# The V projection taken out of the attention groups: a first stage of its own, seven block products per pair of batches

## The chip, the cores and the metric

One core of one Trainium2 chip runs the whole program. TensorE (PE) does the matrix products into PSUM, ScalarE (ACT), VectorE (DVE) and GpSimd (POOL) copy, split and normalise, and SyncE (SP) issues every transfer between the chip's memory (HBM) and SBUF on one queue. The metric is the device time of one execution in microseconds: 1646.34 us is the median of three runs of the kernel before (1646.15 to 1647.33).

## The reference

Two residual layers over 32 batches of 128 x 1024 values in 32-bit floats. The first multiplies each batch by a 128 x 128 matrix picked by an index; the second is causal attention with 16 heads of 64 between four 1024 x 1024 projections.

```python
# x: (32, 128, 1024)
x1 = x + einsum('bct,bcd->bdt', x, L0_weights[conditions])      # layer 1
q, k, v = (einsum('bsd,ed->bse', x1, W) for W in (Wq, Wk, Wv))   # 16 heads of 64
q = q * min(cond_1, 4)                                          # one factor per batch
attn = softmax(where(causal, q @ k.T / sqrt(64), lowest))       # 128 x 128 per head
out = x1 + einsum('bsd,ed->bse', attn @ v, Wo)
```

## The kernel before

**Numbers.** Every product of 32-bit operands is made of three products of split operands: each operand is written as a high part (`XH`, `WH`, ...) and the rest (`XL`, `WL`, ...), and `three()` (L495 to L498) issues high x high, high x low and low x high into one PSUM bank. ACT writes the high part, DVE or POOL subtracts it from the source and so writes the low part.

**Time in steps.** All five engines walk the same list of ticks (`T_START` to `T_OUT`); every operation has a due step in a table (`step_at`, `l0_a`, `kh_ev`, ...), and an engine's program is what falls due on it, in order. A step of the projections is one `three()` with 512 columns: three matmuls of 128 x 512 that contract 128 of the 1024 input columns, so a block (128 output columns, or one batch of V) has 8 steps. The tables set only the order on each engine; what really holds an instruction is its semaphores. A late instruction holds all that stands behind it on its engine.

**Groups.** 8 groups of 4 batches. There are 16 attention stages of 96 steps: stages 0 to 7 do heads 0 to 7 of all groups, stages 8 to 15 heads 8 to 15. A stage has 4 V blocks (one per batch, 512 columns) and 4 pairs of a Q block and a K block (128 columns, two heads, of all four batches at once). The order is Q0 K0 V0 V1 V2 V3 Q1 K1 Q2 K2 Q3 K3; in stages 0 and 8 V comes first. Behind each K block, 5 steps later, stand the scores of its two heads for 4 batches (`p_SC`, 12 matmuls of 128 x 256), and 18 and 20 steps behind that the products with V (`p_PV`, again 12). Between them the softmax runs: DVE adds the mask and takes the maximum, ACT takes the exponential, DVE the reciprocal, POOL normalises, DVE turns P in 10 transposes of 32 x 32 blocks, ACT and POOL split it (`PTH`, `PTL`). I call the 16 steps of a Q and a K block with these 24 small matmuls a cell. Three cells of a stage stand right behind one another; the fourth has the V blocks behind it.

**Layer 1** of group j+1 is spread through stage j: for each half batch three matmuls with the picked matrix (`l0_a`, PE), a copy back (`x_tile`), four transposes (`l0_b`), and the split into `XH`, `XL`. The split x1 of a group is stored once (`X_store`) and read again for stages 8 to 15 (`X_load`). The opening does batch 0 before step 0 and batches 1 to 3 in steps 0 to 24.

**End.** The output projection of group 0 is done plainly (64 steps), that of the other 28 batches in pairs by seven block products instead of eight (28 steps per pair, `pe_product`, `sums`, `w_sum`), with weight sums that are prepared in attention stages (`O_split`, `O_add`).

Of the kernel before, what the change touches and what calls it, by code (L numbers as in the profile page):

```python
# [40 lines left out]
def cond_attention(nc, x, idx, cond, w0, wq, wk, wv, wo, mask_d, ident_d, out):  # L41
# [11 lines left out]
    with ExitStack() as ctx:  # L53
        def sb(name, shape, dt=f32):
            return ctx.enter_context(nc.sbuf_tensor("t_" + name, shape, dt))
# [32 lines left out]
        xr = [sb(f"xr{n}", [128, D]) for n in range(2)]  # L88

        with nc.sbuf_tensor("t_WR", [128, 2, 512], f32) as tile:  # L90
            WR = tile
        xh = sb("xh", [128, 512], f32r)
        xl = sb("xl", [128, 512], f32r)
        with nc.sbuf_tensor("t_WO", [128, 512], f32r) as tile:
            WO = tile
        wr = [sb(f"wr{n}", [128, 128]) for n in range(4)]
        wh = sb("wh", [128, 128], f32r)
        wl = sb("wl", [128, 128], f32r)
        PT = sb("PT", [128, GB, 256])
        PP = sb("PP", [128, GB, 2, 128])  # L100
# [1078 lines left out]
```

## Time and profile before

| | |
|---|---|
| median of 3 runs | 1646.34 us |
| the profiled execution | 1645.11 us |
| its span, first to last instruction | 1643.8 us |
| PE busy | 1630.0 us of the span (99%) |
| DVE / ACT / POOL busy | 912.1 / 746.8 / 588.1 us (55 / 45 / 36%) |
| granted TensorE clock, mean | 0.999 |
| moved by DMA | 221.81 MB, 135 GB/s in the mean |

The span is the time between the first and the last recorded instruction; the device time is 1.3 us more. Matmuls are pipelined: one is shown as 0.39 us long though the next starts 0.23 us later, so the distance from start to start is what a matmul costs. An engine's idle time is listed with what ended it; only PE's can matter much here, since PE carries nearly the whole chain.

### The profile page before, as it was taken

The numbers are of one execution on the slowest core, as the hardware profiler recorded it, in microseconds if no ns is written. First come the engines' busy times: TensorE is split into PE (matmuls) and PEld (weight loads), VectorE is DVE, ScalarE is ACT, GpSimd is POOL, SyncE is SP. The second block draws the span as 40 slices with busy tenths as digits, with TensorE's granted clock in tenths as the row PEclk, the third lists the DMA queues.
The fourth block names the chain that finished last, engine by engine and source line by source line (L and its number), as shares of the span: only waits on it lengthen the run. The fifth ranks groups of instructions, "written<-read, shape, count | busy, mean of one in ns | idle before, by whom it ended". The sixth has DMA issues, their size and how long they took to land.

```text
span 1643.8 us, 22438 instructions
## 1 busy us (share of the span) xinstructions
PE 1630.0 (99%) x7978; PEld 1370.2 (83%) x7978; DVE 912.1 (55%) x1870; ACT 746.8 (45%) x2085; POOL 588.1 (36%) x513
## 2 busy tenths in 40 slices
PE   9999999999999999999999999999999999999999
PEld 7788888888888888878888888888888888888887
DVE  6464646455464637466655556464747455555553
ACT  7464555555454645455444444343545332222221
POOL 2443333434342423342323232222333124555552
PEclk9999999999999999999999999999999999999999
DMA  8442323223141415244424233223221477545442
GB/s 273 179 161 83 149 81 131 97 96 141 60 162 71 167 47 237 65 124 152 150 68 163 90 133 133 92 116 96 116 77 39 167 280 278 178 155 173 171 160 84
DMA packets 91489, 221.81 MB, mean 135 GB/s; under 512 B 8690, under 2 KB 47858, under 8 KB 85234
## 3 DMA queue, kind: packets, MB, share of 16 engines
q1 hardware_dynamic: 91378, 220.38, 37.4%
q8 instruction: 63, 1.03, 0.3%
q14 instruction: 48, 0.39, 0.1%
HBM read 119.69 MB, written 100.66 MB: 134 GB/s over the span
## 4 chain that ended last, share of the span: by engine, by line
PE 93%; DVE 2%; POOL 1%; DMA 1%; ACT 1%; issue 1%; SPq 0%; ACTq 0%; DVEq 0%
PE p_PJ L496 23%; PE p_PJ L497 23%; PE p_PJ L498 23%; PE p_SC L497 4%; PE p_SC L498 4%; PE p_SC L496 4%; PE p_PV L496 2%; PE p_PV L498 2%; PE p_PV L497 2%; PE p_LP L496 2%; PE p_LP L498 2%; PE p_LP L497 2%; PE p_LP L570 1%; DVE t_PT L767 1%; DMA t_wr<-w 1%; POOL t_PTL L909 1%
## 5 line engine op out<-in xcount | busy, mean ns | idle before, releaser
L496 PE MATMUL p_PJ<-t_XH,t_WH 128*128 128x512 f32 x1024 | 404.3, 395 | 0.0
L497 PE MATMUL p_PJ<-t_XL,t_WH 128*128 128x512 f32 x1024 | 400.8, 391 | 0.0
L498 PE MATMUL p_PJ<-t_XH,t_WL 128*128 128x512 f32 x1024 | 399.6, 390 | 0.0
L767 DVE STREAM_TRANSPOSE t_PT<-t_PP 32x256 f32<-32x256 f32 x640 | 278.3, 435 | 16.3 <-POOL t_PP L905 8.2
L909 POOL TENSOR_TENSOR t_PTL<-t_PT,t_PTH 128x512 fp32r<-128x512 f32 x128 | 165.7, 1315 | 339.4 <-ACT t_PTH L710 339.1
L496 PE MATMUL p_PJ<-t_WH,t_XH 128*128 128x512 f32 x708 | 278.0, 393 | 1.3 <-DVE t_XL L792 1.3
L497 PE MATMUL p_PJ<-t_WL,t_XH 128*128 128x512 f32 x708 | 276.3, 390 | 0.0
L498 PE MATMUL p_PJ<-t_WH,t_XL 128*128 128x512 f32 x708 | 275.8, 390 | 0.0
L705 ACT ACTIVATE t_PP<-t_PP,t_st 128x128 f32<-128x128 f32 x512 | 198.7, 390 | 93.3 <-DVE t_st L829 93.3
L905 POOL TENSOR_TENSOR t_PP<-t_PP,t_st 128x512 f32<-128x512 f32 x128 | 133.4, 1044 | 270.7 <-DVE t_st L833 270.5
L498 PEld LDWEIGHTS p_PJ<-t_XH,t_WL 128*128 128x128 f32 x1024 | 192.5, 188 | 41.5
L496 PEld LDWEIGHTS p_PJ<-t_XH,t_WH 128*128 128x128 f32 x1024 | 193.1, 189 | 33.1
L497 PEld LDWEIGHTS p_PJ<-t_XL,t_WH 128*128 128x128 f32 x1024 | 193.5, 189 | 32.6
L498 PEld LDWEIGHTS p_PJ<-t_WH,t_XL 128*128 128x128 f32 x708 | 132.9, 188 | 28.4
L496 PEld LDWEIGHTS p_PJ<-t_WH,t_XH 128*128 128x128 f32 x708 | 133.1, 188 | 25.8 <-issue 1.5
L710 ACT ACTIVATE t_PTH<-t_PT 128x512 fp32r<-128x512 f32 x128 | 74.5, 625 | 176.2 <-DVE t_PT L767 176.2
L497 PEld LDWEIGHTS p_PJ<-t_WL,t_XH 128*128 128x128 f32 x708 | 133.3, 188 | 24.1
L823 DVE SCALAR_TENSOR_TENSOR t_PP<-p_SC,t_beta,t_mask 128x256 f32<-128x256 f32 x256 | 111.6, 477 | 74.5 <-PE p_SC L498 74.5
L803 DVE TENSOR_TENSOR t_KL<-p_PJ,t_KH 64x512 fp32r<-64x512 f32 x128 | 88.2, 689 | 92.9 <-ACT t_KH L689 90.1
L689 ACT ACTIVATE t_KH<-p_PJ 64x512 fp32r<-64x512 f32 x128 | 75.6, 591 | 110.7 <-PE p_PJ L498 108.8
L899 POOL TENSOR_TENSOR t_xl<-t_xr,t_xh 128x512 fp32r<-128x512 f32 x56 | 72.8, 1300 | 121.9 <-ACT t_xh L664 120.8
L792 DVE TENSOR_TENSOR t_XL<-p_LP,t_XH 128x512 fp32r<-128x512 f32 x58 | 40.1, 692 | 103.7 <-ACT t_XH L677 103.4
(210 smaller groups left out, 2528.4 us busy)
## 6 DMA issues: line engine op xcount, KB each, us to landing
xth_scratch<-t_XH SPq DMA_DIRECT2D x8, 2048.0 KB, 6.5
xtl_scratch<-t_XL SPq DMA_DIRECT2D x8, 2048.0 KB, 11.5
at_scratch<-t_AT SPq DMA_DIRECT2D x128, 128.0 KB, 1.8
t_XH<-xth_scratch SPq DMA_DIRECT2D x8, 2048.0 KB, 7.9
t_XL<-xtl_scratch SPq DMA_DIRECT2D x8, 2048.0 KB, 12.5
t_xr<-x SPq DMA_DIRECT2D x30, 512.0 KB, 3.7
...
```

The lines of the kernel that those rows point to most:

```text
L496: pe.matmul(bank, lh, rh, start=first, stop=False, skip_group_check=goes_on)
L497: pe.matmul(bank, lh, rl, start=False, stop=False, skip_group_check=goes_on)
L498: return pe.matmul(bank, ll, rh, start=False, stop=last, skip_group_check=goes_on)
L689: act.activation(KH[r, :, 128 * h:128 * h + 128], pj[r], ACT.Copy).then_inc(act_k, 1)
L705: act.activation(PP[:, u, h, :], PP[:, u, h, :], ACT.Exp, bias=st[:, 0, u, h:h + 1], scale=1.0, accum_out=st[:, 1, u, h:h + 1]).then_inc(a ...
L710: act.activation(PTH[:, u:u + 2], PT[:, u:u + 2], ACT.Copy).then_inc(act_pt, 1)
L767: m = dve.transpose(pt[32 * j:32 * j + 32, :, 32 * i:32 * i + 32], pp[32 * i:32 * i + 32, :, 32 * j:32 * j + 32])
L803: dve.tensor_tensor(KL[r, :, k], pj[r], KH[r, :, k].bitcast(f32), ALU.subtract).then_inc(dve_k, 1)
L823: dve.scalar_tensor_tensor(out=PP[:, u], in0=SC[u // 2][:, 256 * (u % 2):256 * (u % 2) + 256].rearrange("p (h k) -> p h k", h=2), scalar=b ...
L899: pool.tensor_tensor(xl[:], x_tile(bb)[:, h * 512:(h + 1) * 512], xh[:].bitcast(f32), ALU.subtract).then_inc(pool_xl, 1)
L905: pool.tensor_tensor(pp, pp, r, ALU.mult).then_inc(pool_n, 1)
L909: pool.tensor_tensor(PTL[:, u:u + 2], PT[:, u:u + 2], PTH[:, u:u + 2].bitcast(f32), ALU.subtract).then_inc(pool_pt, 1)
```

## The change

V of all heads and batches is now computed in a stage of its own, together with layer 1, before any attention. Its results are split and stored to HBM (`vh_d`, `vl_d`), and so is the split x1. Batches 0 to 3 are done plainly (64 steps, 8 blocks, `pe_plain_v`). The other 28 batches go in 14 pairs: two batches by the two halves of the input columns are a 2 x 2 block matrix, Wv another, and seven block products of 4 steps give what took eight (`pe_v_step`). Four sums of x blocks per pair are made on POOL (`pool_x_sum`) and split by ACT and DVE; four sums of Wv blocks are made once on DVE (`T_add`, from a second load of Wv) and split in steps 24 to 64. Results are gathered from PSUM by ACT and DVE into `GA` and `VR`, split into `VOH`, `VOL` and stored.

After 456 steps come 16 attention stages of 64 steps, four cells each and no V blocks. They load the V of their half of the heads (`V_load`, 2 MB a stage) and x1 (`X_load`, now 14 loads of 4 MB). Stage 0 takes the group that the V stage left in SBUF, stage 8 the one of stage 7. The Q and K weights are split in the V stage (first halves, `p_split`, two pieces in each of pairs 4 to 11) and in cells of the attention (second halves), stored, and loaded when needed (`W_load`). The splits of the output weights are spread over cells 19 to 57; their sums stand 6 steps ahead of their splits instead of 3. The end is the same.

```diff
-STEPS = 96
-T_END = NGRP * STEPS
+STEPS = 64
+PAIR = 28
+NP = B // 2
+T_SEV = 64
+T_ATT = T_SEV + PAIR * (NP - 2)
+T_END = T_ATT + NGRP * STEPS
+GROUP = (7, 0, 1, 2, 3, 4, 5, 6, 6, 7, 0, 1, 2, 3, 4, 5)
...
+        for p in range(2, NP):
+            t = T_SEV + PAIR * (p - 2)
+            plan_l0_pair(2 * p, t - 30)
+            plan_l0_pair(2 * p + 1, t - 16)
...
+        for c in range(4):
+            T_load.put((10, 13, 31, 50)[c], c)
+            for i in range(4):
+                t = (24, 33, 43, 59)[c] + i
+                T_add.put(t, (c, i))
+                T_high.put(t + 1, (c, i))
+                T_low.put(t + 2, (c, i))
+        for p in range(2, NP):
+            t = T_SEV + PAIR * (p - 2)
+            X_store.put(t - 4, p)
+            for i in range(4):
+                Z_add.put(t + (-4.5, -3, -1.25, 0.25)[i], (p, i))
+                S_high.put(t + (-1.25, 2.5, 9.5, 13.5)[i], (p, i))
+                S_low.put(t + (-0.25, 3.5, 10.5, 14.5)[i], (p, i))
+            for i in range(7):
+                for d in range(4):
+                    P_at.put(t + 4 * i + d, (p, i, d))
+            r_at.put(t + 4.25, p)
+            for i, d in enumerate((8, 16, 20, 24, 28)):
+                g_at.put(t + d + 0.25, (p, i))
+            for i, d in enumerate((12, 21, 25, 29)):
+                n = 2 * GB + 4 * (p - 2) + i
+                vh_ev.put(t + d + 0.25, n)
+                vl_ev.put(t + d + 1, n)
+                v_store.put(t + d + 2, n)
...
+        W_load.put(T_ATT - 23.5, (0, 0))
+        W_load.put(T_ATT - 15.5, (1, 0))
+        W_load.put(T_ATT + 5, (1, 1))
...
+        def pe_v_wait(p, i):
+            k = p - 2
+            if i in (0, 2, 5):
+                pe.wait_ge(dve_X, 4 * p + {0: 1, 2: 2, 5: 4}[i])
+            else:
+                pe.wait_ge(dve_S, 4 * k + {1: 1, 3: 2, 4: 3, 6: 4}[i])
...
+            elif i == 2:
+                pe.wait_ge(act_r, k + 1)
+            elif i in (3, 5, 6):
+                pe.wait_ge(dve_g, 5 * k + {3: 1, 5: 2, 6: 3}[i])
+            if k == 0 and i in (1, 3, 4, 5):
+                pe.wait_ge(dve_TL, 16)
+
+        def pe_v_step(p, i, d):
+            if d == 0:
+                pe_v_wait(p, i)
+            lh, ll = v_operand(p, i)
+            mm = three(v_bank(p, i)[:], lh[:, d], ll[:, d], WSH[i][:, d, :], WSL[i][:, d, :], i in (0, 1, 4) and d == 0, d == 3, i in (2, 3, 5, 6))
+            if d == 3:
+                mm.then_inc(pe_P, 1)
...
+        def sp_load_sums(c):
+            if c >= 2:
+                sp.wait_ge(dve_TL, (4, 12)[c - 2])
+            for place in range(4):
+                r0, c0 = 512 * (place // 2) + 128 * c, 512 * (place % 2)
+                sp.dma_start(raw_wv(c)[place], wv[r0:r0 + 128, c0:c0 + 512]).then_inc(l_T[c == 1], 16)
```

How the order moves on three engines. PE, a V block with half a batch of layer 1 among it, in attention stage 1 before (a V step names `t_WH,t_XH`, layer 1 names `p_LP`):

```order
L496 MATMUL p_PJ<-t_WH,t_XH 128x512
L497 MATMUL p_PJ<-t_WL,t_XH 128x512
L498 MATMUL p_PJ<-t_WH,t_XL 128x512
L496 MATMUL p_LP<-t_xh,t_wh 128x512
L497 MATMUL p_LP<-t_xl,t_wh 128x512
L498 MATMUL p_LP<-t_xh,t_wl 128x512
L496 MATMUL p_PJ<-t_WH,t_XH 128x512
L497 MATMUL p_PJ<-t_WL,t_XH 128x512
L498 MATMUL p_PJ<-t_WH,t_XL 128x512
```

and the end of block product 2 and the start of product 3 (counted from 0) of a pair of the V stage now (`t_SH`, `t_SL` are the split sums of x blocks, `t_WSH`, `t_WSL` the split Wv blocks and sums):

```order
L636 MATMUL p_SC<-t_WSH,t_XH 128x512
L637 MATMUL p_SC<-t_WSL,t_XH 128x512
L638 MATMUL p_SC<-t_WSH,t_XL 128x512
L636 MATMUL p_SC<-t_WSH,t_SH 128x512
L637 MATMUL p_SC<-t_WSL,t_SH 128x512
L638 MATMUL p_SC<-t_WSH,t_SL 128x512
L636 MATMUL p_LP<-t_xh,t_wh 128x512
L637 MATMUL p_LP<-t_xl,t_wh 128x512
L638 MATMUL p_LP<-t_xh,t_wl 128x512
```

The forms are the same; the whole list of PE has 7769 rows before and 7601 now (four transposes in a row are one row of it in both).

DVE, before, from the last V block of stage 0 on:

```order
L810 TENSOR_TENSOR t_VL<-p_PJ,t_VH 128x512
L797 TENSOR_TENSOR t_WL<-t_W,t_WH 128x512
L792 TENSOR_TENSOR t_XL<-p_LP,t_XH 128x4x128
L806 TENSOR_TENSOR t_QL<-p_PJ,t_QH 128x512
L792 TENSOR_TENSOR t_XL<-p_LP,t_XH 128x4x128
L803 TENSOR_TENSOR t_KL<-p_PJ,t_KH 64x4x128 x2
```

and now, from step 55 to the first pair (step 64), with the last sums of Wv blocks (`t_TS`) and their splits:

```order
L1025 TENSOR_TENSOR t_XL<-p_PV,t_XH 128x4x128
L1033 COPY t_XR<-p_PV 128x4x128
L1098 TENSOR_TENSOR t_TS<-t_TS 128x512 x3
L1102 TENSOR_TENSOR t_WSL<-t_TS,t_WSH 128x512
L1098 TENSOR_TENSOR t_TS<-t_TS 128x512
L1102 TENSOR_TENSOR t_WSL<-t_TS,t_WSH 128x512 x2
L1083 TENSOR_TENSOR t_SL<-t_SUM,t_SH 128x512
L1102 TENSOR_TENSOR t_WSL<-t_TS,t_WSH 128x512
L1086 TENSOR_TENSOR t_VOL<-p_PJ,t_VOH 128x512
```

Where a few splits stood between PE's blocks, the last eight operations on Wv sums stand close together just ahead of the first pair.

SP, before, in stage 2, a group's store of x1 among stores of attention results:

```order
L1114 DMA at_scratch<-t_AT 128x256 x2
L1099 DMA xth_scratch<-t_XH 128x4096
L1100 DMA xtl_scratch<-t_XL 128x4096
L1114 DMA at_scratch<-t_AT 128x256
L956 DMA t_xr<-x 128x1024
```

and now in the V stage, around the store of a pair's x1 (1 KB pieces in HBM rows of 16 KB):

```order
L1308 DMA xth_scratch<-t_XH 1024x1x256
L1308 DMA xtl_scratch<-t_XL 1024x1x256
L1315 DMA vh_scratch<-t_VOH 128x512
L1316 DMA vl_scratch<-t_VOL 128x512
L1331 DMA t_PR<-wq 128x512
L1502 DMA x_scratch<-t_XT 128x1024
L1281 DMA t_XT<-x 128x1024
L1315 DMA vh_scratch<-t_VOH 128x512
L1316 DMA vl_scratch<-t_VOL 128x512
```

The loads of the next batches and of the weights to split now stand behind stores of 2 MB of x1 and 0.5 MB of V.

## Rows read from the trace of the kernel before

**Rows 1.** The page: busy time of PE and the chain that ended last.

```profile
PE 1630.0 (99%) x7978; PEld 1370.2 (83%) x7978; DVE 912.1 (55%) x1870; ACT 746.8 (45%) x2085; POOL 588.1 (36%) x513
PE 93%; DVE 2%; POOL 1%; DMA 1%; ACT 1%; issue 1%; SPq 0%; ACTq 0%; DVEq 0%
```

**Rows 2.** Waits of PE, whole span: waiting line, releaser, us total, times, longest.

```profile
PE p_PV L496 <- POOL t_PTL L909: 4.4, 10, 1.4
PE p_LP L496 <- POOL t_xl L899: 2.0, 1, 2.0
PE p_PJ L496 <- DVE t_XL L792: 1.3, 1, 1.3
PE p_LP L496 <- DVE t_XL L792: 1.2, 2, 0.8
```

**Rows 3.** Timeline of PE in Q and K blocks: start, duration, instruction; 38 matmuls left out.

```profile
1306.85 0.40 PE L496 MATMUL p_PJ<-t_XH,t_WH 128*128 128x512 f32 x1
...
1315.70 0.39 PE L496 MATMUL p_PJ<-t_XH,t_WH 128*128 128x512 f32 x1
```

**Rows 4.** Timeline of PE in the opening: step 0 and step 32.

```profile
12.92 0.47 PE L496 MATMUL p_PJ<-t_WH,t_XH 128*128 128x512 f32 x1 [1.34 <-DVE t_XL L792]
...
41.88 0.39 PE L496 MATMUL p_PJ<-t_XH,t_WH 128*128 128x512 f32 x1
```

**Rows 5.** Windows: length, busy PE, PEld, DVE, ACT, POOL, clock, DMA share, GB/s.

```profile
10.00:15.00 5.00, 3.48 (x19) 2.62 (x18) 3.52 (x6) 4.62 (x10) 0.91 (x3) 1.00 1.05 393
25.00:30.00 5.00, 5.00 (x27) 4.15 (x27) 3.51 (x6) 3.67 (x8) 0.46 (x1) 1.00 0.69 215
35.00:40.00 5.00, 5.00 (x24) 4.16 (x23) 4.29 (x6) 3.51 (x7) 2.17 (x3) 1.00 0.93 247
55.00:60.00 5.00, 3.00 (x11) 2.10 (x10) 1.98 (x3) 3.19 (x7) 2.18 (x3) 0.84 0.36 126
1365.00:1385.00 20.00, 20.00 (x90) 16.56 (x89) 8.43 (x13) 4.47 (x8) 5.78 (x6) 1.00 0.84 322
943.38:957.20 13.82, 13.82 (x74) 11.88 (x73) 9.62 (x24) 7.53 (x26) 4.63 (x5) 1.00 0.53 223
```

**Rows 6.** The chain in order of time: the load of one picked matrix.

```profile
42.38 12.76 DMA t_wr<-w
```

**Rows 7.** Timeline of SP's queue, the stores issued ahead of it.

```profile
38.06 0.43 SPq L1099 DMA_DIRECT2D xth_scratch<-t_XH  x1
38.53 0.43 SPq L1100 DMA_DIRECT2D xtl_scratch<-t_XL  x1
```

**Rows 8.** Instructions by line and form: busy us, mean ns, idle before.

```profile
L792 DVE TENSOR_TENSOR t_XL<-p_LP,t_XH 128x512 fp32r<-128x512 f32 x58 | 40.1, 692 | 103.7 <-ACT t_XH L677 103.4
L853 DVE TENSOR_TENSOR t_XL<-t_Y,t_XH 128x512 fp32r<-128x512 f32 x28 | 18.0, 685 | 0.2
L853 DVE TENSOR_TENSOR t_XL<-t_WR,t_XH 128x512 fp32r<-128x512 f32 x14 | 19.7, 1444 | 8.7 <-ACT t_XH L744 8.7
L677 ACT ACTIVATE t_XH<-p_LP 128x512 fp32r<-128x512 f32 x58 | 34.7, 598 | 59.0 <-PE p_LP L570 58.1 <-POOL t_WL L948 1.0
L899 POOL TENSOR_TENSOR t_xl<-t_xr,t_xh 128x512 fp32r<-128x512 f32 x56 | 72.8, 1300 | 121.9 <-ACT t_xh L664 120.8
L933 POOL TENSOR_TENSOR t_PP<-t_PP 128x512 f32<-128x512 f32 x7 | 12.1, 1721 | 0.1
L915 POOL TENSOR_TENSOR t_xr<-t_xr 128x512 f32<-128x512 f32 x16 | 21.1, 1321 | 9.3 <-DVE t_xh L849 6.8 <-DVE t_xl L849 1.3
```

**Rows 9.** Timeline of POOL in a cell between two cells.

```profile
957.20 2.54 POOL L909 TENSOR_TENSOR t_PTL<-t_PT,t_PTH 128x512 fp32r<-128x512 f32 x2 [8.12 <-ACT t_PTH L710]
960.31 1.04 POOL L905 TENSOR_TENSOR t_PP<-t_PP,t_st 128x512 f32<-128x512 f32 x1 [0.57 <-DVE t_st L833]
```

**Rows 10.** Timeline of PE: the product with V that takes this `PTL`.

```profile
958.96 0.28 PE L496 MATMUL p_PV<-t_PTH,t_VH 128*128 128x256 f32 x1
```

More of the change, by code:

```diff
@@ new lines, in cond_attention, with slot @@
+        WSH, WSL = [None] * 7, [None] * 7
+        def slot(n, where):
+            WSH[n] = sb(f"WSH{n}", [128, 4, 512], f32r, where)
+            WSL[n] = sb(f"WSL{n}", [128, 4, 512], f32r, where)
+        with ExitStack() as early:
+            for n in range(3):
+                slot(n, early)
+            with nc.sbuf_tensor("t_W0a", [128, DC, 512], f32) as tile:
+                W0 = [tile]
+            slot(3, early)
+        WH, WL = [], []
+        for n in range(2):
+            WH.append(sb(f"WH{n}", [128, DC, 512], f32r))
+            WL.append(sb(f"WL{n}", [128, DC, 512], f32r))
@@ L84, in cond_attention @@
+        WEH = sb("WEH", [128, 4, 512], f32r)
+        WEL = sb("WEL", [128, 4, 512], f32r)
+        PT = sb("PT", [128, GB, 256])
+        xr = [sb(f"xr{n}", [128, D]) for n in range(2)]
+        PP = sb("PP", [128, GB, 2, 128])
         with nc.sbuf_tensor("t_LATE", [128, 4, 512], f32) as tile:
@@ L87, in cond_attention @@
         KL = sb("KL", [128, GB, 256], f32r)
[L88 to L100, printed above, removed]
+        QH = sb("QH", [128, T], f32r)
+        QL = sb("QL", [128, T], f32r)
         PTH = sb("PTH", [128, GB, 256], f32r)
@@ L222, in cond_attention @@
+        for n in range(2 * GB):
+            block("v", n)
+            for d in range(DC):
+                step_at.put(8 * n + d, ("v", n, d))
+            vh_ev.put(8 * n + 8, n)
+            vl_ev.put(8 * n + 8.75, n)
+            v_store.put(8 * n + 9.75, n)
         for d in range(DC):
@@ new lines, in cond_attention, with quiet @@
+        for p in range(2):
+            X_store.put((27, 48)[p], p)
+        def quiet(cell):
+            return T_ATT + 16 * cell + 21 + 9.5
+        p_load, p_split, W_load = At(), At(), At()
+        for m in range(16):
+            t = T_SEV + PAIR * (2 + m // 2) + (10.5, 23.25)[m % 2]
+            p_load.put(t - 9, m)
+            p_split.put(t, m)
+        for m in range(16, 32):
+            p_load.put(quiet(1) - 22 + 11 * (m - 16) if m < 18 else quiet(m - 16) + 2.5, m)
+            p_split.put(quiet(m - 14), m)
@@ L798, in dve_program @@
+                for m in p_split(tick - TICK):
+                    raw, high, low = qk_piece(m)
+                    dve.wait_ge(act_p, m + 1)
+                    dve.tensor_tensor(low, raw, high.bitcast(f32), ALU.subtract).then_inc(dve_p, 1)
                 for n in kl_ev(tick):
@@ new lines, in sp_load_W @@
+        def sp_load_W(n, part):
+            cols = slice(0, 512) if n % 2 == 0 else slice(256 * part, 256 * part + 256)
+            for low in range(2):
+                if n == 0 and low == 0:
+                    sp.wait_ge(s_p, 32 * 16)
+                if n < 2 and part == 0:
+                    sp.wait_ge(pe_P, 7 * (NP - 3) + 2 * n + low + 1)
+                elif n == 2 and low == 0:
+                    sp.wait_ge(pe_q, 4 * NG)
+                elif n == 3 and part == 0 and low == 0:
+                    sp.wait_ge(pe_k, 4 * NG)
+                to = (WH, WL)[low][n % 2][:, :, cols].bitcast(f32)
+                sp.dma_start(to, qk_half(n, low, cols)).then_inc(l_W_rest[n // 2] if part else l_W[n], 16)
@@ L1033, in sp_load_pair @@
         def sp_load_pair(q):
[L1034 to L1035 removed]
+            g, b = divmod(batches(q)[0], GB)
             if q == 0:
```

971 lines of the change are left out of this document (610 added, 361 removed).

## The prediction

> **What bounds the kernel now.** I read the page's busy times and its chain first: PE is busy 1630.0 us of 1643.8 and carries 93% of the chain, no other engine is over 55% [rows 1]. Then PE's waits: only some 9 us in the whole span [rows 2]. So the time is the number of matmuls times their distance. That is read from start to start, not from the 0.39 us shown: 39 matmuls in 1315.70 - 1306.85 = 8.85 us, 0.227 us for one of 128 x 512 [rows 3]; a step of three is 0.681 us. The opening gives the price of layer 1: 32 steps and batches 1 to 3 took 41.88 - 12.92 = 28.96 us [rows 4], less 32 x 0.681 = 21.79 leaves 2.39 us a batch. A cell of Q, K, scores and V products takes 13.82 us [rows 5], 10.9 of them in its 16 steps. The windows also show the clock: full, except 0.84 in the 5 us in which PE stood still for 2.0 us. Last come the queue (rows 6 and 7) and what the other engines have room for [rows 8 to 10].
>
> **What goes.** Steps: 1536 + 64 + 392 = 1992 before, 64 + 392 + 1024 + 64 + 392 = 1936 now. 56 x 3 = 168 matmuls of 0.227 us: **-38.1 us**. Each of 14 pairs has 84 in place of 96; nothing covers them, PE is the chain. Layer 1, scores, V products and the end keep their matmuls.
>
> Waits that go: the 4.4 us of V products for `PTL`, mostly where V or weight splits stood in DVE's and POOL's way; the 2.0 us of layer 1 for `xl` in the opening with about 0.8 us of clock behind it (0.16 of a 5 us window); the 1.2 us for `XL` banks, of which there are two now [rows 2, 5]. **-8 us** together; at the least 0, if others take their place. The 2.0 us came from the queue: the load of one picked matrix took 12.76 us to land [rows 6], since two stores of 2 MB were issued 4 us ahead of it [rows 7]. It is issued 21 steps ahead of its product now, not 12.
>
> **What comes, in the V stage.** A pair has 28 steps and two batches of layer 1: 84 x 0.227 + 2 x 2.39 = 23.8 us. The others must do in that time:
> - ACT: 4 `xh`, 4 copies back, 4 `XH`, 2 raw copies, 1 gather, 4 sums, 4 V, at most 2 weight pieces, 25 x 0.60, and two small ones: 15.6 us.
> - DVE: 4 `XL`, 2 raw, 5 gathers, 4 sums, 4 V, 2 pieces, 21 x 0.69 = 14.5 us; nine of these take both inputs from SBUF.
> - POOL: 4 `xl` of 1.30, 4 sums of 1.32 to 1.72 and small ones: 12.5 to 14 us [rows 8].
>
> All fit. The tightest links are those between products in one bank, 4 steps = 2.7 us for a gather of 0.69; ahead of it DVE has at most an `XL` and a raw copy, 1.4. And product 1 has 4 steps after the sums' chain of POOL, POOL, ACT, DVE. I count 1.5 us for odd delays in 14 pairs; none at best; if every pair lost 1 us, 14.
>
> DVE's two-input operations have two prices here, 685 ns and 1444 ns for the same form, the long one in the stretch where POOL computes sums beside it [rows 8]. If all nine pay the long price, DVE has 14.5 + 9 x 0.76 = 21.3 us in 23.8: it still fits, but every link gets thinner. I take 14.5 to 18, since POOL is busy about half the time; the long price is part of the first rival. The Trainium skill (SBUF — State Buffer, on the shared port pair) says that a VectorE instruction with two SBUF inputs contends with a GpSimd instruction that reads SBUF; by it the 21.3 us would be the rule wherever POOL has work, and the rows of 1444 ns agree.
>
> **The sums of Wv, once.** They come just ahead of the first pair, and product 1 of that pair waits for all 16 splits, at step 68. The last load (1 MB) is issued at step 50, behind a store of 2.1 MB of x1 and one of 0.5 MB of V. At 322 GB/s at 0.84 busy, so 383 at full [rows 5], the 3.6 MB take 9.5 us, at 0.83 us a step to step 61.5 or 62. Behind it DVE has eight operations on sums and one more, nine of 0.69 = 6.2 us = 9 steps: step 71. PE is then 3 to 4 steps late: **+2.6 us**, and a clock loss like the one above, +0.8. Bounds: nothing, if the load lands by 59; 6 us, if the queue is as slow as in the window of 247 GB/s at 0.93.
>
> **The queue.** Per pair: x 1.05 MB, picked matrices 0.13, x1 stores 1.05, split x1 2.10, V 2.10, and in 8 pairs the weight pieces 1.57: 8.0 MB there, 6.4 in the other six. The rate at full share is 374 to 383 GB/s in two windows (393 at 1.05, 322 at 0.84), 312 in one (215 at 0.69) and 266 in the worst (247 at 0.93) [rows 5]. The form new here, 1 KB pieces stored, isn't in the trace; those windows are my bounds. I take about 350, nearer to the mass of rows: 22.9 us for 8.0 MB, under 23.8. The backlog is then largest after the x1 store, some 3 MB or 9 us; an x load issued there lands 10 steps later and is due after 12. So it is hidden, narrowly. The Trainium skill (DMA: Bandwidth & Descriptors, Bandwidth) lists 341 GB/s for a transfer of 1 MB and asks for at least 1 MiB each; here V goes in pieces of 256 KB. With its 341 the pair's bytes would take 23.5 us, hidden as well.
>
> **The start of attention.** The first Q block needs 4.2 MB of weights, issued at steps 4.5 and 8 of the last pair behind some 2 MB: 6.3 MB at 383 are 16.5 us = 24 steps of 0.681, due at 28. The K weights are due 8 steps later and have 8.4 MB ahead and with them. Both nearly on time: **+1 us**; 0 to 6.
>
> **The cells.** All 64 are now back to back. The trace has that already: three in each stage follow one another, and there `PTL` is ready at 957.20 + 1.27 = 958.47 and taken at 958.96, 0.5 us to spare [rows 9, 10], with DVE busy 9.6 of 13.8 us [rows 5]. So the cadence holds without V. In 16 cells a sum of output weights (1.32 us on POOL, [rows 8]) now stands ahead of the normalising at 960.31, which has a gap of 0.57 before it [rows 9]: 0.75 us late there, 0.25 at the second one, within 0.5. Weight splits fall in gaps of DVE. **+1 us**; 0 to 16 x 0.75 = 12. X, 4.2 MB, and V, 2.1 MB, per stage of 55 us are 115 GB/s: no load there.
>
> **Sum**, from the profiled execution's own 1645.1 us: -38.1 - 8 + 1.5 + 3.4 + 1 + 1 = -39.2, so 1605.9. Its time is 1.2 us under the median of the runs, inside their spread; I say **1606 us**.
>
> **The rivals.**
> 1. *The V stage is paced by more than PE, mildly* (queue at 312 GB/s or DVE by the shared port). 8.0 MB at 312 are 25.6 us, 1.8 over PE's, in 8 pairs 15 us: about 1620. For it: a backlog of 9 us in every pair, in-order engines, loads due 2 steps after they land. Against: the faster windows, and six pairs that need only 270 GB/s.
> 2. *The cells lose their 0.5 us.* If each cell waits 0.5 us more for `PTL`, since nothing between stages lets DVE catch up: 64 x 0.5 = 32 us, 1638. For it: ten such waits before. Against: the third cell in a row before had the same spacing as the second, 13.8 us.
> 3. *Slower than before: the queue at its worst rate.* At 266 GB/s 8.0 MB take 30.1 us, 6.3 over, times 8 = 50, and 6.4 MB take 24.2, 2 more in six pairs: 1658. It decides from 277 GB/s downward, where 8 x 5.1 us eat the 40. For it: one 5 us window, with pieces of 2 KB and 512 B. Against: it is a stretch of loads waiting for one another as much as a rate.
> 4. *No change*: the seven products save nothing because PE waits in every pair for the gathers, 2.8 us of the 23.8. Every link has over 1 us to spare, so I see no place for it.
>
> **How the numbers follow.** Forecast 0.64 (its own range 1599 to 1613), rival 1 0.18, rival 2 0.09, rival 3 0.06, rival 4 0.03. The range from 1598 to 1634 leaves out rivals 3, 4 and most of 2, and a little below: 0.2. A measurement here tells 0.2% (3.3 us) from no change: faster 0.91, same 0.02, slower 0.07.
>
> **What would show it.** PE's list 168 matmuls shorter and PE still at 98% or more; pairs of 23.8 us; the attention at 64 x 13.82 = 884 us with waits for `PTL` of 0.3 us here and there; one wait of 2 to 4 us at product 1 of the first pair, at about 70 us, with a dip of the clock. In the V stage the DMA share should stand at 0.85 to 0.95 for 8 pairs. I am wrong if PE waits there once per pair, for `xl`, `xh` or a gather behind a late load (rivals 1 and 3), or if the distance of cells is over 14.1 us (rival 2).

## The result, and the profile after

| | before | after |
|---|---|---|
| median (4 runs each, same chip) | 1646.84 us (1646.15 to 1649.08) | 1631.25 us (1630.27 to 1631.86) |
| span of the profiled execution | 1643.8 us | 1629.4 us |
| granted TensorE clock, mean | 0.999 | 0.995 |
| moved by DMA | 221.81 MB | 353.99 MB |

The ratio is 0.9902, 95% interval 0.9885 to 0.992: 15.6 us faster, where 40 were forecast. The time lies in the range of 1598 to 1634, in its upper end; in size the forecast is 25 us off.

The page of after, busy times and chain:

```profile
PE 1595.2 (98%) x7810; PEld 1340.5 (82%) x7810; DVE 1068.2 (66%) x2072; ACT 808.7 (50%) x2199; POOL 662.3 (41%) x554
PE 79%; DMA 6%; SPq 6%; DVE 3%; issue 2%; POOL 2%; ACT 2%; ACTq 0%; DVEq 0%
```

Against [rows 1] the list is 168 matmuls shorter, as said, and 34.8 us less busy. But the chain has 79% PE where it had 93: DMA and SP's queue carry 12% of it. PE's waits, whole span (against [rows 2]):

```profile
PE p_PJ L636 <- DVE t_VOL L1086: 5.1, 1, 5.1
PE p_LP L770 <- ACT t_XT L897: 4.8, 4, 3.1
PE p_PJ L636 <- DMA t_WL<-wl_scratch: 4.8, 1, 4.8
PE p_PV L636 <- DVE t_VR L1051: 4.2, 3, 2.0
PE p_PV L636 <- POOL t_PTL L1240: 2.3, 3, 1.1
PE p_PJ L636 <- DVE t_VR L1051: 2.0, 2, 1.7
PE p_PJ L636 <- ACT t_GA L905: 1.9, 3, 0.6
...
PE p_SC L636 <- ACT t_GA L905: 1.5, 3, 0.6
```

The waits that were to go are gone but for 2.3 us of `PTL`. In their place stand others, nearly all before or at the start of the attention. Without a wait it would begin at 13.74 + 456 x 0.681 + 31 x 2.39 = 398.4 us; its first matmul starts at 426.85. **28.5 us are lost in three places**, read as the distance from start to start above its price; the places below were read one by one, so their sum is not exactly that.

*The opening, 11 us.* PE around the last steps before the first pair, and its product 1:

```profile
74.04 0.39 PE L638 MATMUL p_PJ<-t_WSH,t_XL 128*128 128x512 f32 x1
77.49 0.66 PE L770 MATMUL p_LP<-t_ident,t_XT 128*128 128x128 f32 x4 [3.06 <-ACT t_XT L897]
83.27 0.77 PE L636 MATMUL p_PJ<-t_WSH,t_SH 128*128 128x512 f32 x1 [5.12 <-DVE t_VOL L1086]
83.84 0.63 PE L637 MATMUL p_PJ<-t_WSL,t_SH 128*128 128x512 f32 x1
84.26 0.63 PE L638 MATMUL p_PJ<-t_WSH,t_SL 128*128 128x512 f32 x1
```

The waits give 0.9 + 3.2 + 5.4 us in distances, and the matmuls behind stand 0.43 us apart up to 86: 1.4 us more, at the lower of the two clock levels (1.2 GHz). The cause of both waits is seen in SP's queue and on DVE and ACT: the load of Wv's last quarter is issued at 64.79 and awaited until 74.14, and the copies of x stand behind the sums on ACT.

```profile
64.79 2.66 SPq L1302 DMA_DIRECT2D t_TS<-wv  x4
```

```profile
74.14 2.15 DVE L1098 TENSOR_TENSOR t_TS<-t_TS 128x512 f32<-128x512 f32 x3 [6.58 <-DMA t_TS<-wv]
...
77.41 2.63 DVE L1102 TENSOR_TENSOR t_WSL<-t_TS,t_WSH 128x512 fp32r<-128x512 f32 x2
79.96 1.75 DVE L1083 TENSOR_TENSOR t_SL<-t_SUM,t_SH 128x512 fp32r<-128x512 f32 x1
...
82.49 0.68 DVE L1086 TENSOR_TENSOR t_VOL<-p_PJ,t_VOH 128x512 fp32r<-128x512 f32 x1
```

```profile
74.87 2.08 ACT L918 ACTIVATE t_WSH<-t_TS 128x512 fp32r<-128x512 f32 x3 [8.65 <-DVE t_TS L1098]
```

From the landing to the end of `t_VOL` DVE takes 9.0 us for ten operations. Those that take both inputs from SBUF took up to 1.75 us each while POOL was at work beside them (77.8 to 81.2 us); all others took about 0.7. Product 1 also waits for this `t_VOL`, the last plain V block, whose bank it writes. It stands behind the sums on DVE, and product 1 starts 0.10 us after its end, at 83.17.

*The pairs, 13 us.* All from 182 to 327 us, in pairs that carry weight pieces: twelve waits, 9.8 us, eleven of them 11.4 in distances, and some 2 at the lower clock near 327. Pairs there take 25.5 us (five pairs in 310.19 - 182.48), not 23.8. *The start of the attention*: 4.84 us for the low first weights, 5.0 in distance, and another 1.9 behind it at the lower clock. Windows of after, columns as in [rows 5]:

```profile
40.00:60.00 20.00, 20.00 (x94) 16.56 (x93) 19.35 (x26) 11.32 (x21) 6.37 (x6) 1.00 1.04 333
60.00:80.00 20.00, 14.31 (x68) 11.15 (x66) 11.39 (x18) 10.50 (x22) 10.89 (x10) 0.99 1.07 363
80.00:100.00 20.00, 16.73 (x73) 13.80 (x74) 10.76 (x16) 9.11 (x19) 7.19 (x7) 0.84 0.63 200
182.48:327.11 144.63, 134.85 (x624) 107.92 (x623) 87.59 (x118) 77.44 (x151) 75.98 (x66) 1.00 0.98 310
420.00:440.00 20.00, 15.16 (x58) 12.06 (x58) 2.61 (x5) 1.77 (x4) 0.00 (x0) 0.83 0.88 306
```

Line four is the main reading: for 145 us the 16 DMA engines are 98% busy and move 310 GB/s. 8.0 MB a pair at 310 are 25.8 us, what a pair takes. No engine is near its limit there: DVE 88 us of 145. How a late transfer reaches PE is seen on ACT, which takes its work in order. Its longest waits from 182 to 327 us are for the weight pieces and for the picked matrices (`t_wr`, which POOL prepares):

```profile
ACT t_PRH L924 <- DMA t_PR<-wk: 17.1, 5, 6.1
ACT t_wh L892 <- POOL t_wr L1220: 11.4, 6, 2.8
ACT t_PRH L924 <- DMA t_PR<-wq: 9.2, 2, 4.6
```

What stands behind such a wait is late, and DVE behind it: ahead of PE's 2.0 us at 224 us ACT waited 4.6 us for a piece and 2.8 for a matrix, and DVE 5.1 us for ACT. The full queue is seen in SP too: with much outstanding an issue takes 1.2 us and not 0.4, and SP becomes late itself.

```profile
254.97 1.26 SPq L1339 DMA_DIRECT2D wl_scratch<-t_PRL  x1
256.28 1.23 SPq L1315 DMA_DIRECT2D vh_scratch<-t_VOH  x1
257.55 1.24 SPq L1316 DMA_DIRECT2D vl_scratch<-t_VOL  x1
258.83 1.18 SPq L1331 DMA_DIRECT2D t_PR<-wk  x1
```

*The attention* keeps its cadence; the answer to [rows 9], POOL of a cell and of the next one, 13.81 us later:

```profile
1012.29 2.54 POOL L1240 TENSOR_TENSOR t_PTL<-t_PT,t_PTH 128x512 fp32r<-128x512 f32 x2 [8.12 <-ACT t_PTH L952]
1015.40 1.04 POOL L1236 TENSOR_TENSOR t_PP<-t_PP,t_st 128x512 f32<-128x512 f32 x1 [0.57 <-DVE t_st L1136]
...
1026.10 2.54 POOL L1240 TENSOR_TENSOR t_PTL<-t_PT,t_PTH 128x512 fp32r<-128x512 f32 x2 [8.12 <-ACT t_PTH L952]
```

### The profile page after: what moved, and what is told of

Its sections match the earlier page's. It is cut to its first block, busy times and chain, and to the rows that moved or that the text cites. A ratio compares the mean times of both kernels' runs of the same rounds, so it can differ in the third digit from the quotient of the medians.

```text
span 1629.4 us, 22999 instructions
## 1 busy us (share of the span) xinstructions
PE 1595.2 (98%) x7810; PEld 1340.5 (82%) x7810; DVE 1068.2 (66%) x2072; ACT 808.7 (50%) x2199; POOL 662.3 (41%) x554
## 2 busy tenths in 40 slices
DMA packets 171815, 353.99 MB, mean 217 GB/s; under 512 B 13234, under 2 KB 97458, under 8 KB 161458
## 4 chain that ended last, share of the span: by engine, by line
PE 79%; DMA 6%; SPq 6%; DVE 3%; issue 2%; POOL 2%; ACT 2%; ACTq 0%; DVEq 0%
PE p_PJ L636 19%; PE p_PJ L637 19%; PE p_PJ L638 18%; PE p_SC L637 4%; PE p_SC L636 4%; PE p_SC L638 4%; PE p_PV L636 2%; PE p_PV L637 2%; PE p_PV L638 2%; DMA t_wr<-w 2%; DMA at_scratch<-t_AT 2%; DMA t_WL<-wl_scratch 1%; SPq L1316 1%; PE p_LP L637 1%; PE p_LP L636 1%
## 5 line engine op out<-in xcount | busy, mean ns | idle before, releaser
L636 PE MATMUL p_PJ<-t_XH,t_WH 128*128 128x512 f32 x1008 | 395.5, 392 | 4.8 <-DMA t_WL<-wl_scratch 4.8
L638 PE MATMUL p_PJ<-t_XH,t_WL 128*128 128x512 f32 x1008 | 392.9, 390 | 0.0
L947 ACT ACTIVATION_READ_ACCUMULATOR t_PP<-t_PP,t_st 128x1 f32 x512 | 95.9, 187 | 0.0
L1132 DVE TENSOR_REDUCE t_st<-t_PP 128x2 f32<-128x256 f32 x256 | 94.2, 409 | 0.0
L1228 POOL TENSOR_TENSOR t_xl<-t_XT,t_xh 128x512 fp32r<-128x512 f32 x56 | 79.8, 1425 | 5.4 <-ACT t_xh L840 5.2
L1220 POOL TENSOR_TENSOR t_wr<-t_wr,t_ident 128x128 f32<-128x128 f32 x32 | 21.6, 676 | 143.6 <-DMA t_wr<-w 143.6
L1136 DVE RECIPROCAL t_st<-t_st 128x4 f32<-128x4 f32 x128 | 22.8, 178 | 87.2 <-ACT t_PP L947 87.2
L636 PE MATMUL p_PV<-t_PTH,t_VH 128*128 128x256 f32 x256 | 72.1, 282 | 2.3 <-POOL t_PTL L1240 2.3
L638 PE MATMUL p_PV<-t_PTH,t_VL 128*128 128x256 f32 x256 | 72.3, 282 | 0.0
L638 PE MATMUL p_SC<-t_KH,t_QL 128*128 128x256 f32 x256 | 72.2, 282 | 0.0
```

What stands on the lines that cost most here:

```text
L636: pe.matmul(bank, lh, rh, start=first, stop=False, skip_group_check=goes_on)
L638: return pe.matmul(bank, ll, rh, start=False, stop=last, skip_group_check=goes_on)
L947: act.activation(PP[:, u, h, :], PP[:, u, h, :], ACT.Exp, bias=st[:, 0, u, h:h + 1], scale=1.0, accum_out=st[:, 1, u, h:h + 1]).then_inc(a ...
L1132: dve.tensor_reduce(st[:, 0, u, :], PP[:, u], AX, ALU.max, negate=True).then_inc(dve_m, 1)
L1228: pool.tensor_tensor(xl[h][:], x_tile(bb)[:, h * 512:(h + 1) * 512], xh[h][:].bitcast(f32), ALU.subtract).then_inc(pool_xl, 1)
```

## Experiments

Each run has four timed executions of the kernel (e10 has ten), and before beside it on the same chip (medians 1646.1 for e1 to e4, 1645.0 for e5 to e8, 1646.3 for e9 to e12, 1647.8 for e13 to e16). The number to beat is after's 1631.3. "Waits in the pairs" are PE's from 180 to 330 us, 9.8 us in after.

**e1: the first weights in halves.** As K's do, Q's first 2 x 2 MB come in two parts of 2 x 1 MB each.

```diff
+        W_load.put(T_ATT + 3, (0, 1))
         W_load.put(T_ATT + 5, (1, 1))
```

> The first Q weights (4.2 MB, 512 columns) are loaded as two halves of 256 columns, the second half 3 steps after the start of attention; all else as in the changed kernel, whose span is 1629.4 us with a wait of 4.84 us at that start and some 2 us of half clock behind it. Queue theory: what is due at that moment is halved, the wait and the clock loss go, about 1624 us (-7). Rival: the transfer in front of it (stores of V and x1) is what is late, and the wait only moves to the K weights or shrinks to 3 us: 1628 to 1630.

1634.5 us (1631.6 to 1638.1), ratio 0.9932 (0.991 to 0.9954). The wait for `t_WL` fell to 0.7 us, and one of 3.5 us for low V came 29 us later:

```profile
428.92 0.47 PE L638 MATMUL p_PJ<-t_XH,t_WH 128*128 128x512 f32 x1 [0.66 <-DMA t_WL<-wl_scratch]
...
457.37 0.36 PE L638 MATMUL p_PV<-t_PTH,t_VH 128*128 128x256 f32 x1 [3.49 <-DMA t_VL<-vl_scratch]
```

The time lies above both forecasts: no gain. What was let past PE's first need was paid at its next.

**e2: the low half of V is not stored.**

```diff
-            sp.dma_start(vl_d[half][g][:, cols], VOL[n % 2][:].bitcast(f32)).then_inc(s_V[n % 2], 16)
```

> The low part of V is computed but not stored, and the load of it takes the high part, so the result is off; every engine's arithmetic is as in the changed kernel and a pair has 1.05 MB less in the queue (7.0 and 5.4 MB for 8.0 and 6.4), the opening 2.1 MB less. Queue theory (bytes at some 320 GB/s): the waits of the first pair (9 us), of the 8 pairs with weight pieces (12 us) and half of that at the start of attention go, with their clock losses: 1605 to 1612 us. Engine theory (ACT, DVE and POOL have too much to do in order): the waits stay, 1627 to 1631.

1609.2 us (1608.6 to 1609.6), ratio 0.9772 (0.9755 to 0.9788). With 1.05 MB of 8.0 less in a pair, and all work of the engines kept, PE waits for nothing from 180 to 330 us:

```profile
180.00:330.00 150.00, 150.00 (x710) 123.92 (x709) 101.52 (x133) 88.85 (x170) 88.02 (x76) 1.00 0.86 290
```

6.95 MB in 23.8 us are 292 GB/s, which the queue gives at 0.86 busy. The engines' work is kept, so that work is not what holds the pairs. But SyncE also has 4 of a pair's 22 issues less, so e2 alone does not part bytes from issues. The 22 us are most of the miss of 25; what it still loses is the opening (4.9 us for `VOL` again).

**e3: the weight pieces are not split.** Loaded and stored twice as they are; no ACT, no DVE.

```diff
-            sp.wait_ge(act_p, m + 1)
-            sp.dma_start(wh_d[m // 8][:, cols], high.bitcast(f32)).then_inc(s_p, 16)
+                sp.wait_ge(l_p[m % 2], 16 * (m // 2 + 1))
+                sp.dma_start(wh_d[m // 8][:, cols], raw).then_inc(s_p, 16)
...
-                sp.wait_ge(dve_p, m)
+                sp.wait_ge(s_p, 32 * m)
```

> The first 16 Q and K weight pieces are loaded and stored twice as they are, without ACT's copy and DVE's subtraction (the result is off); bytes and transfers are the same. Engine theory: ACT and DVE are freed of the two operations per pair and of ACT's waits for the piece (30 us in all), the 12 us of waits in the 8 pairs go, 1617 to 1620 us. Queue theory: at most a little, 1627 to 1632, since the loads of x and of the picked matrices come as late as before.

1635.3 us (1634.5 to 1636.6), ratio 0.993. DVE does 79 us of work in the 150 instead of 92, and PE still waits 7.6 us there:

```profile
180.00:330.00 150.00, 142.31 (x647) 113.74 (x645) 78.98 (x107) 73.91 (x145) 77.20 (x69) 0.98 0.90 304
```

Less work on the engines brought no gain, as the queue theory has it. The test is not clean, though: since the raw tile is now stored itself, SyncE holds its queue before each load of a piece until the last stores have landed (the last two lines of the edit). After has no such wait, and with it the DMA share fell to 0.90:

```profile
SPq L1335 <- DMA wl_scratch<-t_PR: 33.4, 12, 3.5
```

So it is e2, not e3, that rules out DVE's load and its shared port as what holds the pairs.

**e4: the split x1 stored in pieces of 8 KB.** As many bytes, from another tile that lies contiguous. The load of the first weights waits for these stores.

```diff
-            for tile, to in ((XH[0], xth_d), (XL[0], xtl_d)):
+            for tile, to in ((WSH[0], xth_d), (WSL[0], xtl_d)):
```

> The store of a pair's split x1 (2 x 1 MB) takes its bytes from a tile that lies in one piece (8 KB per partition on both sides, in place of 8 pieces of 1 KB), so the values stored are others; bytes, order and waits are the same. Piece-size theory: the queue gains speed, DMA share in the 8 pairs falls from 1.0 to some 0.85 and most waits go, 1608 to 1615 us. Byte theory: rate and waits stay, 1627 to 1632.

1622.9 us (1621.8 to 1623.4), ratio 0.9853 (0.9837 to 0.9869). Between both: larger pieces for 2.1 of the 8.0 MB are worth 8 us; 324 GB/s, and 3.9 us of waits in the pairs.

```profile
180.00:330.00 150.00, 145.98 (x685) 118.53 (x683) 97.22 (x127) 85.42 (x165) 86.28 (x74) 1.00 0.96 324
```

**e5: the sixteen pieces spread over pairs 1 to 12.** `PLACE` is a table of pair and half for each piece.

```diff
-            t = T_SEV + PAIR * (2 + m // 2) + (10.5, 23.25)[m % 2]
+            t = T_SEV + PAIR * PLACE[m][0] + (10.5, 23.25)[PLACE[m][1]]
```

> The sixteen weight pieces (0.8 MB each: read, then stored as high and low) come one or two to a pair over pairs 1 to 12, instead of two in each of pairs 4 to 11; nothing else changes. Theory (the queue gives some 320 GB/s, and a pair with two pieces has 8.0 MB for it, 25.0 us of queue in 23.8 us): eight pairs had to pay some 13.5 us; with one piece a pair has 7.2 MB, 22.5 us, and pays nothing, and the four pairs that keep two (2, 6, 9 and 12) stand apart, so their backlog is worked off. 1620 to 1625 us, and PE's waits for t_GA and t_VR, 9.6 us in the changed kernel, fall to under 3. Rival (a piece's own conversions on ScalarE and VectorE hold the evictions; there are as many of them as before): 1629 to 1633.

1628.6 us (1626.2 to 1630.2), ratio 0.9888. The waits in 180 to 330 us fell to 3.7, but the wait for the first weights grew from 4.8 to 6.3 us, since the queue is now fuller up to the end of the stage (0.93 busy from 330 to 420 us, 0.86 in after). Part of the gain was given back there: a miss of 4 us.

**e6: sums of Wv's quarters 0 to 2 on GpSimd, X of pair 1 stored at step 56.**

```diff
+                for c, i in T_add(tick):
+                    if c < 3:
+                        T_sum(pool, pool_TA, 4 * c + i, c, i)
...
-            X_store.put((27, 48)[p], p)
+            X_store.put((27, 56)[p], p)
```

> The sums of Wv's quarters 0 to 2 go from VectorE to GpSimd, two steps apart and begun 3 steps earlier; those of quarter 3 stay; and the X of the second pair is stored at step 56, behind the load of quarter 3, not at step 48 ahead of it. Theory (VectorE, busy 19.35 of 20 us at 40 to 60, and the late quarter 3 set the end of the sums, and TensorE waits 5.1 us for them at product 1 of the first pair, 3.1 us for X's evictions ahead of it, and then runs at the lower clock for 3 us): 8 to 10 us of the 10.9 go, and 1622 to 1625 us. Rival 1 (only the load of quarter 3 counts, and comes late as before behind the rest of the queue): the wait stays at 3 to 5 us, 1629 to 1632. Rival 2 (GpSimd's sums of 128x512 take so long, or hold VectorE back so much, that they are late themselves): the wait grows, 1633 to 1640.

1632.9 us (1630.0 to 1634.6), ratio 0.9918: no gain, between rivals 1 and 2. POOL was 19.8 of 20 us busy at 40 to 60, the load of quarter 3 was issued at 67.0 (64.8 in after), and product 1 waited 5.3 us.

**e7: high V stored from ScalarE's queue.** Same bytes, same pieces, another issuer.

```diff
                 for n in vh_ev(tick):
                     act_v_high(n)
+                    act.wait_ge(act_v, n + 1)
+                    act.dma_start(vh_d[half][g][:, b * 512:(b + 1) * 512], VOH[n % 2][:].bitcast(f32)).then_inc(s_V[n % 2], 16)
```

> The stores of V's high half are issued by ScalarE, behind its own eviction, and no longer by SyncE; bytes and pieces are the same. Theory (bytes and pieces set the rate; that SyncE's issues grow from 0.35 to 1.2 us is only the sign of a full queue): 1629 to 1635 us, the waits stay within 2 us of the 9.6 us for t_GA and t_VR, and ScalarE's issues get long in their turn. Rival (the length of the issues on one sequencer sets what is stored late): with 128 of some 300 issues off SyncE the waits for t_GA and t_VR fall below 4 us, and the time to 1618 to 1625.

1622.9 us (1621.8 to 1623.7), ratio 0.9856 (0.9827 to 0.9884). The theory that bytes and pieces alone set the rate fell; the rival's number came. The rate rose to 331 GB/s at the same busy share (309 to 315 at 0.97 to 0.99 in after and in e1, e6, e9, e12 and e15, each once), the waits in the pairs fell to 2.2 us, and no issue of ScalarE's was over 0.35 us, while SyncE's stayed long:

```profile
180.00:330.00 150.00, 147.79 (x696) 120.33 (x695) 98.12 (x129) 89.77 (x171) 89.56 (x76) 1.00 0.98 331
```

```profile
253.02 0.33 ACTq L915 DMA_DIRECT2D vh_scratch<-t_VOH  x1
```

```profile
258.28 1.32 SPq L1319 DMA_DIRECT2D vl_scratch<-t_VOL  x1
```

The edit changes three things at once: the issuer, the hardware queue that carries these bytes (queue 10 with 11.6% of the DMA engines' time, where after has all on queue 1), and the moment, for a high half now goes without waiting for VectorE's low half. The runs do not tell them apart. If 4 issues fewer on SyncE are worth at most these 8 us in e2 as well, at least 14 of its 22 are its bytes (an estimate).

**e8: e5, e6 and e1 together.**

> Three edits together: the pieces spread over pairs 1 to 12, the Wv sums of quarters 0 to 2 on GpSimd with the second pair's X stored later, and the first attention weights loaded in halves. If the first two losses stand apart, as the theory has it, their gains add: 1631.3 less 8 for the spread, less 8 for the sums, nothing for the halves, is 1615, range 1611 to 1619. If one backlog of the queue runs through all of it (what is not lost in the opening is lost in the pairs, for the queue is what is full from 40 us on): 1622 to 1630.

1628.7 us (1625.1 to 1631.6), ratio 0.9893: no more than e5 alone, in the range of the one backlog. Two of the three gave nothing by themselves, so it says little on whether gains add.

**e9: the X of the last pair stored in the attention.** SyncE waits for it before the X load of stage 2.

```diff
-            X_store.put(t - 4, p)
+            X_store.put(T_ATT + 12 if p == NP - 1 else t - 4, p)
```

> The X of the last pair (2 MB) is stored 12 steps into the attention, behind the loads of the first attention weights, of V and of X of the next group, and no longer 4 steps ahead of its pair's products. Theory (at the start of the attention the queue is a line: what stands ahead of the first weights' low half delays it; 2.1 MB at 340 GB/s are 6.2 us, more than the 4.8 us that TensorE waits): the wait for t_WL goes, the 2 us at the lower clock behind it too, 6 to 7 us less than the changed kernel run beside it. Rival (the wait moves on to the load of low V, as it did when the weights were loaded in halves, 3.5 us there): 2 to 4 us less. Rival (nothing: the weights are late from their buffers, not from the queue): within 1.5 us.

1629.6 us (1625.4 to 1631.3), ratio 0.9895. The wait for the weights fell from 4.84 to 1.68 us, and no lower clock followed (1.00 from 420 to 440, 0.83 in after); `PTL` then cost 1.1 at 483 us and as much once more before 900, where e12 has none. The median gains 2.1 us over e12 beside it, less than the 6 to 7 of the theory; the intervals overlap.

```profile
423.35 0.47 PE L636 MATMUL p_PJ<-t_XH,t_WH 128*128 128x512 f32 x1 [1.68 <-DMA t_WL<-wl_scratch]
```

**e10: X of pairs 0 and 1 stored behind the loads of Wv.**

```diff
-            T_load.put((10, 13, 31, 50)[c], c)
+            T_load.put((10, 13, 30, 49.5)[c], c)
-                t = (24, 33, 43, 59)[c] + i
+                t = (24, 33, 42, 59)[c] + i
-            X_store.put((27, 48)[p], p)
+            X_store.put((34, 56)[p], p)
```

> In the opening the X of pairs 0 and 1 is stored at steps 34 and 56, behind the loads of Wv's quarters 2 and 3, not at 27 and 48 ahead of them (2 MB each), and quarter 2's sums one step earlier. Theory (the chain load 2, sums 2, load 3, sums 3 sets product 1 of the first pair; each load waits behind 2 MB of X in the queue, 9 to 10 us from issue to landing where 1 MB alone would take 3): load 2 lands some 3 us earlier, load 3 as much or more, and of the 8.6 us of waits at 74 to 83 us 4 to 7 go: 4 to 8 us less than the changed kernel beside it. Rival (VectorE's own line of sums, 19.4 of 20 us busy at 40 to 60, is the limit, and each load waits for it through its buffer): 0 to 2 us less.

1637.9 us (1632.7 to 1644.9), ratio 0.9951: slower than after by 6. Pair 2's x takes the tile that pair 0's store reads. With that store later its low part is late, and layer 1 stands still ahead of a wait of 5.0 us that stayed:

```profile
63.00 0.76 PE L636 MATMUL p_LP<-t_xh,t_wh 128*128 128x512 f32 x1 [5.99 <-DVE t_XL L1025]
```

**e11: e5, e7, e9 and e10 together.**

> Four edits together: the last X stored late, X stored behind Wv's loads in the opening, high V stored from ScalarE's queue, and the weight pieces spread over pairs 1 to 12. If the three places are losses of their own: 6 for the start of the attention, 5 for the opening, and 10 to 12 of the 13.5 in the pairs, so 21 to 23 us less than the changed kernel beside it, 1607 to 1611 us, which is what the kernel would take if the queue cost nothing but the opening's rest. If they share one backlog, and relief at one place is paid at the next: 1615 to 1621.

1623.8 us (1622.2 to 1625.3), ratio 0.986: with e10's loss in it.

**e12: the changed kernel again**, the measure for e9 to e11.

> The changed kernel itself, unedited, on the chip of the other three, so that edits worth 3 to 7 us are read against it and not over two chips: 1631 us, 1628 to 1634.

1631.7 us (1631.0 to 1634.4), ratio 0.9915 (0.9899 to 0.9932), with the three places as in after: 4.9 us at product 1, 5.0 for the weights.

**e13: e5, e7 and e9.**

> The four edits of the kernel with all cures, but for the one in the opening, which cost 6.2 us by itself against the changed kernel beside it: so the last X stored late, high V stored from ScalarE's queue, and the weight pieces spread. If the edits' gains add (2 us, 8 to 9 us and 3 us by themselves): 1617 to 1619 us. If the spread and ScalarE's queue cure the same thing: 1620 to 1623.

1620.2 us (1617.8 to 1621.1), ratio 0.9828 (0.9808 to 0.9848): the median fits the second forecast, the runs reach into both. 1.0 us of waits is left in the pairs, 2.4 at the weights. The spread and ScalarE's queue seem to cure much the same loss: e7 alone had left 2.2.

```profile
180.00:330.00 150.00, 149.02 (x701) 121.36 (x699) 96.25 (x127) 87.19 (x167) 90.42 (x78) 1.00 0.94 313
```

**e14: e13, and X of pair 1 at step 56.**

> The three cures, and the X of pair 1 alone stored at step 56, behind the load of Wv's quarter 3; that of pair 0 stays at step 27, since its delay made ScalarE and VectorE wait for X's tile. Theory (quarter 3 lands 9.4 us after its issue since 2 MB of X stand ahead of it in the queue): 2 to 4 us less than the three cures alone. Rival (the load is issued late, when the quarter before has left its buffer, and that is what counts): within 1.5 us of them.

1618.0 us (1616.3 to 1618.4), ratio 0.9821 (0.9802 to 0.9839): **the fastest but e2, which leaves stores out**, and 13 us under after. It is 2.2 under e13, in the theory's range, though the runs overlap. Quarter 3 lands 6.8 us after its issue and product 1 starts at 81.0, where e13 has 9.0 and 84.8. The wait at product 1 stayed at 4.9 us, since what comes ahead of it got earlier too, and since DVE now takes 10.3 us from the landing to `t_VOL`. PE, then DVE:

```profile
75.52 0.66 PE L771 MATMUL p_LP<-t_ident,t_XT 128*128 128x128 f32 x4 [0.41 <-ACT t_XT L898]
81.04 0.77 PE L637 MATMUL p_PJ<-t_WSH,t_SH 128*128 128x512 f32 x1 [4.86 <-DVE t_VOL L1091]
```

```profile
70.69 3.63 DVE L1103 TENSOR_TENSOR t_TS<-t_TS 128x512 f32<-128x512 f32 x3 [2.13 <-DMA t_TS<-wv]
75.11 1.75 DVE L1103 TENSOR_TENSOR t_TS<-t_TS 128x512 f32<-128x512 f32 x1
```

**e15: quarter 3 of Wv not loaded**, its sums made from what lies there, 7 steps earlier.

```diff
-            T_load.put((10, 13, 31, 50)[c], c)
+            if c < 3:
+                T_load.put((10, 13, 31)[c], c)
-                t = (24, 33, 43, 59)[c] + i
+                t = (24, 33, 43, 52)[c] + i
```

> The changed kernel without the load of Wv's quarter 3: its sums, conversions and products are all made, 7 steps earlier, from what lies in the buffer (so V is not that of the reference). Theory (the way from quarter 2's end in the buffer over the load of quarter 3, issued at 64.8 and landed at 74.1 us, to its sums sets product 1 of the first pair): the waits of 3.1 and 5.1 us and the 2 us of low clock behind them go, 1621 to 1624 us. Rival (VectorE has no room for the sums ahead of the first pair, whenever the data come): a wait of 3 us or more stays, 1626 to 1631.

1626.3 us (1624.5 to 1628.1), ratio 0.9871 (0.985 to 0.9892). The load is half of the story. PE, then POOL:

```profile
79.31 0.47 PE L637 MATMUL p_PJ<-t_WSH,t_SH 128*128 128x512 f32 x1 [2.48 <-DVE t_SL L1084]
```

```profile
74.06 1.29 POOL L1192 TENSOR_TENSOR t_SUM<-t_XR 128x512 f32<-128x512 f32 x1 [6.08 <-issue]
75.43 1.28 POOL L1195 TENSOR_TENSOR t_SUM<-t_SUM,t_XR 128x512 f32<-128x512 f32 x1
```

With Wv's sums done at 72.7 product 1 still waits 2.5 us, now for the chain POOL, POOL, ACT, DVE on x, which begins when the last x is copied at 73.9 and ends on DVE at 78.6, 4.7 us behind. `t_VOL` follows it, and product 1 starts 0.10 us after its end at 79.21, as in after. In after it is hidden behind the wait for Wv.

**e16: e13 with the high X stored from ScalarE too.**

> The three cures, and the stores of X's high half (1 MB each, 16 of them) issued by ScalarE as well. If it is the one sequencer's long issues that limit the rate (309 GB/s in 180 to 330 us with all on SyncE, 331 with 24 of 150 issues on ScalarE): 1 to 3 us less than the three cures. If ScalarE's waits for the queue now hold its evictions: 1 to 5 us more.

1620.4 us (1618.1 to 1621.6), ratio 0.9837: the same as e13. One wait of 1.4 us for `GA` came in the pairs; the rest is alike. More issues on ScalarE gave nothing at 0.93 to 0.94 busy; with the pieces not spread and the queue at 0.98 it was not tried.

## Why the prediction was off

**Held:** 168 matmuls and with them the 38.1 us; PE at 98%; most of the waits that go; the cadence of the cells (13.81 us, 2.8 us of distances lost in all 64, +1 forecast), so rival 2 falls; no loss by DVE's load or the shared port in the pairs (e2). Two-input operations did get dearer, 1059 ns in the mean for `t_VOL<-t_VR` against 686 for `t_VOL<-p_PJ`, inside the 14.5 to 18 us counted for DVE. The dip of the clock came where it was put, and at two places more (near 327 and behind 427 us). The sign named for being wrong came true as well: in six pairs PE waited eleven times for gathers behind late loads, as rival 1 has it.

**The step that failed is the queue's rate**, "I take about 350, nearer to the mass of rows". After's 145 us at 0.98 moved 310 GB/s. That is the 312 of the one window [rows 5] and the figure of rival 1, with 15 us for it; the pairs lost 13. I had weighed windows by their number. None of them held this mix: the one of 374 held loads only, most of them of 256 KB, the one of 383 loads of 0.25 to 1 MB and stores of 256 KB, and the worst, 266, two stores of 2 MB of x1. e4 (larger pieces for a quarter of the bytes: 324 GB/s, 8 us less) and e7 (high V by ScalarE: 331 GB/s, 8 us less) show two things that the rate hangs on: the size of the pieces, and that all came from one issuer and queue. Why the second counts is open. The page of the Trainium skill that I cited (DMA: Bandwidth & Descriptors, Bandwidth) has 341 GB/s at 1 MB transfers, for loads. Here most were of 256 or 512 KB, stores among them, and the highest rate of these 150 us in any run was e7's 331.

**The Wv term, 3.4 us forecast, 11 measured.** The arrival was put at step 61.5; the load was issued at 64.8 us, since it needs the buffer of the quarter before, and landed 9.4 us later. I had reckoned the transfer (9.5 us) but not when the chain load 2, sums 2, load 3 would let it be issued, nor that ACT's copies of x stand behind it. Behind it DVE was given nine operations of 0.69 us, 6.2 in all (at the text's own 0.83 us a step that is 7.5 steps, not 9). It took 9.0, with one operation more and the long price of two inputs from SBUF, which I had left out here. e15 shows a second line of 5 us behind it that the text knew of ("product 1 has 4 steps", 2.7 us) and did not add up.

**The start of the attention, 1 us forecast, 7 measured**, 1 us beyond the bound of 6. The 6.3 MB were given 16.5 us; from the issue at 409.06 us to the low weights 17.6 us passed, most of it in one transfer, here from the chain that ended last:

```profile
410.29 16.43 DMA t_WL<-wl_scratch
```

The larger part is the issue's date: due 23.5 steps, 16.0 us, ahead of the first Q block, it came 12.8 us ahead (at 409.06 for 421.85), behind SyncE's stores of V. e9 shows the term: without the 2.1 MB of X ahead of them the wait is 1.7.

These are 7.6 + 11.7 + 6 = 25.3 us over their terms (11, 13.2 and 7 measured; 3.4, 1.5 and 1 forecast), and the forecast was 25.3 under the median. That the two agree so well is partly luck: the first V step came 0.8 us later than before, and the cells lost 1.8 more than forecast, and neither is in the sum. And that the time lies in the range at all is owed to the room left for rivals. Rival 1's own number, 1620, has the pairs right and misses the other two places. *Open*: e2, e13 and e14 still wait 5 us in the opening. Two versions were not tried: one that loads Wv's last quarter into a buffer of its own, and one with the last plain `t_VOL` ahead of the sums.
